# Second layer's feed-forward stage: attention scores and values by tiles of 32 queries and 64 keys, with the shared rotation adds

## What is computed

```python
xs = shift_half_of_features_by_one_token(x)
q, k, v = split(xs @ Wqkv)                 # 128 -> 3 x 1024: 16 heads of 64
q, k = l2norm(rotate(q)), l2norm(rotate(k))
s = q @ k.T * scale + band                 # token t sees keys t-32 .. t
x = x + softmax(s) @ v @ Wo                # 1024 -> 128
h = layernorm(shift(x))
x = x + (h @ W1_value * gelu(h @ W1_gate)) @ W2   # 341 hidden features
```

## Time and profile before

| | us |
|---|---|
| median of 3 runs | 2709.92 (2708.59 to 2713.13) |
| span of the profiled execution | 2709.9 |
| of it: PE busy | 2399.8 (89%) |
| DVE busy | 1612.7 (60%) |
| ACT busy | 1232.8 (45%) |
| POOL busy | 1033.8 (38%) |
| the stage (24 units) | some 754 to 1912 of the span |

### The profile page before, as it was taken

One profiled execution on the slowest core, in us unless ns is written; L12 is line 12 of the kernel. 1 busy time (PEld: TensorE's weight loads), 2 busy tenths in 40 slices (PEclk: granted clock), 3 DMA queues, 4 the chain that ended last, 5 costly groups with the idle time before them and its releaser, 6 DMA issues. The chain is left out here.

```text
span 2709.9 us, 46097 instructions
## 1 busy us (share of the span) xinstructions
PE 2399.8 (89%) x15951; PEld 1422.1 (52%) x16003; DVE 1612.7 (60%) x3811; ACT 1232.8 (45%) x3219; POOL 1033.8 (38%) x901
## 2 busy tenths in 40 slices
PE   4979998699669999999999999999597996997998
PEld 2446666455435655565665656666355443454443
DVE  3544544476368887878887888876364223473333
ACT  1334452155246676766666666666151111164221
POOL 2010000201178787877787787875101002000000
PEclk7989998898789999999999999999797898698999
DMA  1110000000010000000000000000000110100010
GB/s 59 26 28 1 1 1 1 16 3 2 2 51 5 21 12 15 17 17 14 13 17 25 9 10 25 9 9 1 12 6 0 31 31 5 19 2 25 24 35 20
DMA packets 45348, 42.03 MB, mean 16 GB/s; under 512 B 7421, under 2 KB 35749, under 8 KB 45108
## 3 DMA queue, kind: packets, MB, share of 16 engines
q1 hardware_dynamic: 42612, 36.59, 4.7%
q10 hardware_dynamic: 2496, 2.36, 0.4%
HBM read 33.36 MB, written 0.52 MB: 13 GB/s over the span
## 5 line engine op out<-in xcount | busy, mean ns | idle before, releaser
L3320 POOL TENSOR_TENSOR l1fb_p<-l1fb_p,l1fb_rden 128x640 f32<-128x640 f32 x192 | 240.4, 1252 | 218.7 <-DVE l1fb_rden L3387 218.7
L3312 POOL TENSOR_TENSOR l1fb_rinv<-l1fb_ssq,neghalf 128x8 f32<-128x8 f32 x192 | 319.2, 1662 | 8.5 <-DVE l1fb_ssq L3377 8.4
L3516 PE MATMUL ps<-l1fb_wqkv,l1fb_xs 128*128 128x512 f32 x576 | 298.3, 628 | 9.1 <-DVE l1fb_xs L3343 4.3
L3472 ACT ACTIVATE l1fb_p<-ps,l1fb_shift 128x128 f32<-128x128 f32 (+1 forms) x768 | 281.9, 391 | 0.3
L3314 POOL TENSOR_TENSOR l1fb_qk<-l1fb_qk,l1fb_rinv 128x512 f32<-128x512 f32 x192 | 206.6, 1076 | 15.0
L3479 ACT ACTIVATE l1fb_pT<-ps 128x512 f32<-128x512 f32 x192 | 114.7, 597 | 191.3 <-PE ps L3568 191.3
L3453 ACT ACTIVATE l1fb_sq<-ps 128x512 f32<-128x512 f32 x192 | 114.8, 598 | 170.1 <-PE ps L3516 167.7
L3382 DVE TENSOR_REDUCE l1fb_shift<-ps 128x4 f32<-128x640 f32 x192 | 157.2, 819 | 52.0 <-PE ps L3546 50.0
L3472 ACT ACTIVATION_READ_ACCUMULATOR l1fb_p<-ps,l1fb_shift 128x1 f32 x768 | 167.8, 219 | 0.0
L3568 PE MATMUL ps<-ident,l1fb_p 128*128 128x128 f32 x768 | 125.8, 286 | 39.7 <-ACT l1fb_g L3488 27.3
L3546 PE MATMUL ps<-l1fb_kT,l1fb_qT 64*128 64x128 f32 (+1 forms) x1536 | 147.3, 310 | 0.0
(11 more groups left out here) (711 smaller groups left out, 5398.2 us busy)
## 6 DMA issues: line engine op xcount, KB each, us to landing
l1fb_wqkv<-in_L_ffn_Wqkv SPq DMA_DIRECT2D x24, 256.0 KB, 2.7
l3f_w<-in_L_ffn_W SPq DMA_DIRECT2D x21, 256.0 KB, 3.3
l2f_w<-in_L_ffn_W SPq DMA_DIRECT2D x16, 256.0 KB, 3.1
l1fb_wqkv<-in_L_ffn_Wqkv SPq DMA_DIRECT2D x6, 512.0 KB, 3.9
l1fb_wo<-in_L_ffn_Wo SPq DMA_DIRECT2D x6, 512.0 KB, 4.2
l1fb_w<-in_L_ffn_W SPq DMA_DIRECT2D x6, 341.0 KB, 2.9
l1fb_w<-in_L_ffn_W SPq DMA_DIRECT2D x6, 128.0 KB
x_tok<-in_x SPq DMA_DIRECT2D x1, 512.0 KB
```

The source lines that it names most:

```text
L3312: nc.gpsimd.tensor_tensor(w.rinv[:, u, :], w.ssq[:, u, :], chip.neghalf[:, 0:8], ALU.pow).then_inc(*w.unit_norm.end(f"rinv{u}"))
L3320: nc.gpsimd.tensor_tensor(p, p, w.rden[:, c, :, :].rearrange("p j q -> p (j q)").unsqueeze(2).to_broadcast([P, 2 * QT, SEEN]), ALU.mult)\
L3472: last = nc.scalar.activation(w.p[:, c % 4, j, q, 0:hi - lo], ps[:, SCORE_BANK(c) + j, lo:hi], ACT.Exp, bias=w.shift[:, c, j, q:q + 1], ac ...
L3516: nc.tensor.matmul(ps[:, PROJ_BANK(u), :], w.xs[:, x.odd, q * P:(q + 1) * P], w.wqkv[:, col:col + 512], start=True, stop=True)\
```

## The change

All of it lies in the stage's functions; tokens are cut into eight **windows** of 32 (`WINDOWS`), and a window's queries see the 64 keys from 32 before it.

- Scores: 16 matmuls of 32 queries x 64 keys for a pair of heads (`tile_position` by strip of 64 rows and group of 32 columns) in place of four. The band matmuls shrink to 128 columns, the maxima (`max`) to 256 elements, the exponentials to 64 columns each and without sums. One pair of score banks (0, 1) instead of two.
- Values: 16 matmuls of 32 queries x 65 columns, the 65th a column of ones, so that the softmax sums come out beside the values. They come out queries by features in banks 2 and 3. `att` is then a product of PSUM with the reciprocal sums, and POOL's scaling `s` and DVE's `edge` go.
- Turning: `T` is two transposes of p and two of the att of the pair before; one ACT copy (`c`) brings both into `w.both`, from which `y1` reads. A pair's values therefore follow one round after its turning, and att is turned one round later still.
- The value projection (`p8` to `p11`) is two matmuls of 64 tokens for each of the odd windows; the even windows (the same keys, shifted by 32) are made by four SBUF-to-SBUF transfers a unit on SP's queue (`even_windows`).
- Each feed step's output (`y1`, `mean`, `var`, `spread`, `value`, `y2`) goes to banks 2 and 3, in turn with the values; `gate2` computes the third gate and value together in bank 7. A new step `values_ready` (`G`) holds the waits for V.
- The clamp is a TENSOR_TENSOR with a tile of 1e-24. The memset of p goes; small ones take its place.
- The rotation adds stay as they were: DVE the even, POOL the odd ones.
- The plans are written anew.

```diff
-SCORE_BANK = lambda c: c % 2 * 2
-ITEM_BANK = lambda c: 4 + c % 2
-PROJ_BANK = lambda u: 6 + u % 2 if u < QK else 4 + (u + 1) % 2
-TURN_BANK = lambda n: 4 + (n + 1) % 2
+SCORE_BANK, VALUE_BANK, ITEM_BANK, TURN_BANK = 0, 2, 4, 5
+PROJ_BANK = lambda u: 6 + u % 2
...
-DVE_PLAN = """inv7' att5' max0 edge6' r7' tab    inv0 att6' max1 edge7' g0' g1' r0 g2'  ...
+DVE_PLAN = """inv6' att6' max0 r7' tab    inv7' att7' max1 g2' r0 g0' g1'    ...
...
+            def even_windows(t):
+                sp.wait_ge(*w.vals.done("v11", t))
+                for j in range(2):
+                    v = w.v[DH * j:DH * j + DH, t % 2, :, :, :].rearrange("p w c d -> p w (c d)")
+                    sp.dma_start(v[0:EDGE, 2:WINDOWS:2, :], v[EDGE:DH, 1:WINDOWS - 2:2, :]).then_inc(w.dup_in, 16)
+                    sp.dma_start(v[EDGE:DH, 0:WINDOWS:2, :], v[0:EDGE, 1:WINDOWS:2, :]).then_inc(w.dup_in, 16)
...
-        nc.vector.tensor_scalar(w.ssq[:, u, :], w.ssq[:, u, :], 1e-24, None, ALU.max)...
+        nc.vector.tensor_tensor(w.ssq[:, u, :], w.ssq[:, u, :], fp(w.tiny), ALU.max)...
...
     def attended(x, c):
-        after(eng, w.V, f"V{c}", x)
-        nc.vector.tensor_copy(w.attT[:, x.odd, c, :], ps[:, ITEM_BANK(c), 0:S])...
+        after(eng, w.T, f"T{(c - 1) % ITEMS}", x.past(0 if c else 1))
+        after(eng, w.inv, f"inv{c}", x)
+        nc.vector.tensor_tensor(w.att[:, c % 2, :, :, :].rearrange("p q j d -> p j q d"), by_head()[:, :, :, 0:DH],
+                                w.rden[:, c % 2, :, :].unsqueeze(3).to_broadcast([P, 2, QT, DH]), ALU.mult)...
...
+    def odd_window(x, u):
+        m = u - QK
...
+        for j in range(2):
+            last = nc.tensor.matmul(ps[DH * j:DH * j + DH, TURN_BANK, :]..., w.xs[:, x.odd, SEEN * m:SEEN * m + SEEN],
+                                    weights[:, j, :, :], start=True, stop=True, tile_position=(0, DH * j))
...
+    def values_ready(x, c):
+        after(eng, w.kept, f"c{c}", x)
+        if c == 0:
+            eng.wait_ge(w.dup_in, x.t * 64 + 64)
+        after(eng, w.att_made, f"att{(c - 1) % ITEMS}", x.past(0 if c else 1))
+        if c in (0, 1):
+            after(eng, w.norm, ("g1", "x2")[c], x.past(2))
+        elif c in (2, 3, 4, 6):
+            after(eng, w.norm, {2: "x1", 3: "diff", 4: "vareps", 6: "xn0"}[c], x.past(1))
+
+    def scores(x, c):
+        for n in range(WINDOWS):
+            q, at = n // 4, EDGE * (n % 4)
             for j in range(2):
                 rows = slice(DH * j, DH * j + DH)
+                last = nc.tensor.matmul(ps[at:at + EDGE, SCORE_BANK + j, q * SEEN:(q + 1) * SEEN], w.qT[rows, x.odd, c, EDGE * n:EDGE * (n + 1)],
+                                        w.kT[rows, x.odd, c, EDGE * n:EDGE * n + SEEN], start=False, stop=(q == 1), tile_position=(DH * j, at))
         last.then_inc(*w.S.end(f"S{c}"))
+    def values(x, c):
+        for n in range(WINDOWS):
...
+                last = nc.tensor.matmul(ps[at:at + EDGE, VALUE_BANK + j, q * (DH + 1):(q + 1) * (DH + 1)],
+                                        w.both[rows, ITEMS * x.odd + c, 0, EDGE * n:EDGE * (n + 1)],
+                                        w.v[rows, x.odd, n, c, :], start=True, stop=True, tile_position=(DH * j, at))
...
     def weights_turned(x, c):
-        after(eng, w.scaled, f"s{c}", x)
...
+        after(eng, w.X, f"X{c}", x)
+        after(eng, w.att_made, f"att{(c - 1) % ITEMS}", before)
+        after(eng, w.kept, f"c{(c - 1) % ITEMS}", before)
+        of = ([(0, w.p[:, c % 2, :, :, :])] if x.real else []) + ([(1, w.att[:, (c - 1) % 2, :, :, :])] if before.real else [])
...
```

More of the change, by code:

```diff
@@ L3016 @@
 EDGE = 32
-SEEN = P + EDGE
+SEEN = 2 * EDGE
+WINDOWS = S // EDGE
 def l1_ffn_constants():
@@ L3586, in attended @@
     def attended(x):
-        after(eng, w.att, "att7", x)
+        eng.wait_ge(*w.kept.done("c0", x.past(-1).t))
         eng.wait_ge(w.wo_in, x.layer * 16 + 16)
-        after(eng, w.rot, "rot1", x.past(-2))
+        after(eng, w.att_made, "att1", x.past(-1))
+        after(eng, w.norm, "x2", x.past(1))
         for c in range(ITEMS):
-            last = nc.tensor.matmul(ps[:, 7, 0:S], w.wo[:, c, :], w.attT[:, x.odd, c, :], start=(c == 0), stop=(c == ITEMS - 1))
+            last = nc.tensor.matmul(ps[:, VALUE_BANK, 0:S], w.wo[:, c, :], w.both[:, (ITEMS * x.odd + c + 1) % (2 * ITEMS), 1, :],
+                                    start=(c == 0), stop=(c == ITEMS - 1))
@@ L3615, in gates @@
             after(eng, w.rot, "rot6", x.past(-2))
-        else:
-            after(eng, *((w.turned, "e4", x.past(-2)) if x.past(-2).real else (w.att, "att5", x.past(-1))))
-        for i in ((0, 1) if which == 1 else (2,)):
-            at, n = FFN_CHUNKS[i]
-            dst = ps[0:n, 5, 0:S] if i == 2 else ps[0:n, 6, i * S:(i + 1) * S]
-            last = nc.tensor.matmul(dst, w.w1[:, FFN_IN + at:FFN_IN + at + n], fp(w.diff), start=True, stop=True)
-        last.then_inc(*(w.feed.end("gate01") if which == 1 else w.gate2.end("gate2")))
@@ L3624, in chunk_values @@
[L3624 to L3633 removed]
+            for i in (0, 1):
+                at, n = FFN_CHUNKS[i]
+                last = nc.tensor.matmul(ps[0:n, 6, i * S:(i + 1) * S], w.w1[:, FFN_IN + at:FFN_IN + at + n], fp(w.diff), start=True, stop=True)
@@ new lines, in gates, with chunk_values @@
+            last.then_inc(*w.feed.end("gate01"))
+        else:
+            after(eng, w.rot, "rot7", x.past(-2))
+            at, n = FFN_CHUNKS[2]
+            for i, of in enumerate((FFN_IN, 0)):
+                last = nc.tensor.matmul(ps[0:n, 7, i * S:(i + 1) * S], w.w1[:, of + at:of + at + n], fp(w.diff), start=True, stop=True)
+            last.then_inc(*w.feed.end("gate2"))
+    def chunk_values(x, which):
+        after(eng, w.att_made, "att7", x.past(-1))
+        for i in (0, 1):
+            at, n = FFN_CHUNKS[i]
+            last = nc.tensor.matmul(ps[0:n, VALUE_BANK + i, 0:S], w.w1[:, at:at + n], fp(w.diff), start=True, stop=True)
+        last.then_inc(*w.feed.end("value01"))
```

308 lines of the change are left out of this document (147 added, 161 removed).

## The result

The changed kernel takes 2731.4 us (median of 4 runs, 2724.03 to 2734.55) against 2711.53 before (4 runs beside them): ratio 1.0067, 95% interval 1.0049 to 1.0085. It is slower, by 20 us between the medians and by 18 between the profiled spans. The forecast was 2699 and faster; the measured time lies where the prediction had put its first slower rival (2716 to 2755, chance 0.24), and inside the stated range. The profiled execution's span is 2728.2 us.

A forecast was written before the change was run, and what follows sets the result against it. PE was taken to bound the kernel (95%), DVE close behind (82%). A unit going from 46.57 to 46.2 us gave -9 over 24 units, and smaller memsets -2: 2709.9 to 2699 us, range 2650 to 2780, likeliest 2680 to 2704.

The forecast's parts named there:

- The mechanism: Rounds 0 and 1: one chain across PE, ACT and DVE, 13.35 us, leaving PE still for some 5 us.
- the sum: One unit's rounds added up: 45.05 us, with additions 46.2, against 46.57 before.
- Round 2: PE's work of 5.1 us after the gap, put at 6.9 because of the lower clock.
- At half clock for about 3.5 us of wall time it gets 1.8 less done: Round 2, after PE's gap: the lower clock adds 1.8 us to PE's 5.1.
- Of the adds nothing changes: Rotation adds: DVE keeps the even ones and POOL the odd ones, with no change expected.
- Rounds 6 and 7: Bound by DVE's chain, 8.85 us together; PE has only 6.1 to do.
- The value projections stay at about one projection's time: PE's value projections: no change expected, at about one projection's time; a projection was 0.96 us before.
- Round 5: Bound by DVE's chain: values, inv, att, max, an even rotation and vareps, 4.4 us.
- PE stays the bound: Much faster rival: 35.5 us of PE work plus 1.6, under 38 a unit, near 2500 us; chance 0.04.
- The longer chain: Slower rival: rounds 0 and 1's chain longer, clock falling twice, 46.8 to 48.5 us a unit; chance 0.24.
- The floor of the small matmuls: Slower rival: a minimum time per small V and S matmul, +5.2 us a unit, 2824 us; chance 0.14.
- The clock does not fall: Faster rival: clock kept or DVE's chain overlapping PE's, 43.5 to 45.7 us a unit, 2640 to 2690; chance 0.18.

The follow-up runs named there:

- edit 1: Changed kernel with DVE taking g0' and g1' right after g2', ahead of r0: 2680.33 us, ratio 0.9884 to before.
- edit 2: Changed kernel with ACT taking the squares q0 ahead of X1's table load and exponentials: 2673.45 us, ratio 0.9848 to before.
- edit 3: Changed kernel with g0' and g1' ahead of r0 on DVE and q0 ahead of X1 on ACT: 2658.33 us, ratio 0.9799 to before.
- edit 11: Kernel before the change with only X1 put ahead of q0 on ACT: 2754.98 us, ratio 1.0149 to before.
- edit 4: Changed kernel with five unread 512-column filler matmuls on PE between p1 and G0's wait: 2699.03 us, ratio 0.9951 to before.
- edit 5: Changed kernel with the 16 score matmuls of a pair of heads issued twice into the same banks: 2765.12 us, ratio 1.0193 to before.
- edit 8: Changed kernel with g0' and g1' ahead of r0, and q0 and the copy c0 ahead of X1: 2653.56 us, ratio 0.9777 to before.
- edit 10: Changed kernel with the clamp by a scalar (TENSOR_SCALAR), as before the change: 2731.95 us, ratio 1.0065 to before.

## Why the prediction was wrong, point by point

- **The mechanism** of rounds 0 and 1 was as put: the gap of "some 5 us" ahead of G0 is 4.48, the rounds are 13.37 where the sum had 13.35, and not by luck, since r0 starts 9.83 us into them where the sum had 9.77. The lower clock follows. Edits 1, 2 and 3 show that the order is the cause; edit 11 that its ACT half costs 42 us even in the kernel before.
- **The forecast's sign** fell on sizes behind it. Round 2 was put at 6.9 and is 7.72. The step "At half clock for about 3.5 us of wall time it gets 1.8 less done" failed: the lower level holds for 5.72 us of PE's work and costs 2.40 (edit 4). That is 0.6 of the 0.8; the rest is work, 5.32 for 5.1. No row stood behind the 3.5, and the earlier trace rows had the lower level for all of their 5.00 us.
- **"Of the adds nothing changes"** failed, and with it an odd rotation of 2.06: POOL's add is the same, but it starts sooner, and the clamp behind which DVE's chain goes on takes 0.75. Round 4 was put at 4.25 as PE's; it is 4.94 and DVE's, with the rotation 2.64 and the values 0.80 after the wait where 0.64 was put. Rounds 6 and 7 are 9.54 (8.85), with 2.73 for their odd rotation. As an estimate from these rows, round 4 would be PE's at 4.52 without the longer clamp and rounds 6 and 7 up to 0.6 shorter: 1.0 us a unit, 24 us in all. No run tests it.
- **"The value projections stay at about one projection's time"** failed: two column tiles of 512 take 1.01, not 0.86. t takes 0.56 where 0.44 was carried over: it now follows small tiles. V and S take 0.79 for 0.70. This counts where PE is the bound, in round 3, 7.48 (7.3), and in round 2. Round 5 is 4.57 (4.4), for the values' 0.80 again.
- Of the excess, 2.57 us a unit, the sum had added 1.15: it came to 46.2 and the unit is 47.6.
- **The loop's jump** had no term of its own: it costs 4.4 us beyond an ordinary period where it cost 2.2, 8.6 more in all.
- **Not priced the other way**: the first pass is 6.6 us shorter and not 2, since its rounds have no feed half: 4.05 us each against 5.21. The start that is 3.8 us sooner is chance. So the 29 us from forecast to span are 28 for twenty units at 1.4 each and 8.6 for the jumps, less 4.6 and 3.8, within 1 us.
- **A slip in a side sum**: 44.4 less 8 x (0.12 + 0.96) is 35.8 and not 35.5. Only the rival "PE stays the bound" uses it.
- **The rivals.** The longer chain gave the right time, by half of its mechanism: the second fall of the clock comes only behind the jump, not in each unit, and in its place stand the longer rotations. The floor of the small matmuls is excluded: 32 records of V take 0.27, 0.008 each, and edit 5 has 0.010 for each further one. The Trainium skill's 25 ns from start to start ("TensorE: Matmul & The Clock Gate", section "Wait — 56ns, not 53.3ns?") does not hold for tiles that lie side by side. "The clock does not fall" is what edits 1 and 8 get in part of their units.
- **Edits put at nothing**: the clamp's form was that (edit 10), and so were the transfers, which end no wait of G0. POOL's lost work was not, for it let the add start into the clamp.

## What to carry to other kernels

When work is taken from the bounding engine, read the chain that the new order builds across the other engines: here PE lost 123 us of work and the kernel took 18 us longer, mostly because one squaring stood behind a table load and one product behind a rotation. Putting each consumer of a slow step as early as its inputs allow (two swaps in the plans) turned +0.7% into -2.0%. Price a gap on TensorE with the clock behind it, and look in the trace for what a loop's jump costs. An engine that is relieved of work starts its next step sooner: look at what that step now overlaps.

## What the runs showed of the hardware

- Matmuls of 64 rows by 32 columns of the array on eight tiles, 64 or 65 columns of f32, take 0.008 to 0.010 us a record from start to start (0.27 for 32, and 0.32 for 32 added ones); going from them to full tiles costs about 0.2 us more.
- The granted clock fell to 0.50 within a gap of 4.48 us and stayed there for the first 5.72 us of PE's work behind it. Around gaps of 2.56 to 2.66 (edit 2) it was 0.50 for 3.4 us in each ordinary unit; with gaps of 2.24 (edit 3), of 1.78 (edit 8), or of 1.06 and 1.43 (edit 1) it fell in some units and not in others. Ten records whose result nobody reads, put into the gap, kept it at 1.00.
- With 667 PE records a unit in the loop's body, where there were 307, PE paused within a group of matmuls behind each jump (2.03 us in the rows above), and the jump period was 4.4 us longer than its neighbours against 2.2 before.
- A VectorE instruction on 128x8 elements that started while GpSimd's 128x512 add ran ended 0.02 to 0.03 us behind the add, in all of 91 cases, and took 0.74 to 1.25 us, where the median before, with no add beside it, was 0.17. No run separates the two.
